# Blocks that depend on the context: kept as one float32 copy, split into two parts when they are loaded

## The reference, cut to what matters

```
# layer 0, for each batch
qh = (x @ wq + bq), kh = (ctx @ wk + bk), vh = (ctx @ wv + bv)     # 16 heads of 64
scores  = qh / 8 @ kh.T + 2 * bias
weights = softmax(scores)
out     = layernorm(weights @ vh (all heads side by side) @ wo + bo + x)
# layer 1: h = out + attn(ln(out)); h = h + attn(ln(h), context); h + geglu_ff(ln(h))
```

## Time and profile before

| | us |
|---|---|
| median of 3 runs (lowest, highest) | 3728.07 (3726.77, 3730.91) |
| the profiled execution | 3724.3 |
| span of its core | 3722.5 |
| busy PE / DVE / ACT / POOL | 2985.1 / 2187.8 / 1626.3 / 1329.6 |
| DMA moved in the span | 518.20 MB |

### The profile page before, as it was taken

The page is one execution under the profiler, slowest core; times in us unless marked ns, Lnnn a source line. Parts: engine busy times, 40 slices in busy tenths (PEclk is TensorE's granted clock), DMA queues, the critical chain, the costliest instruction groups (busy, mean ns, idle before and its releaser), DMA issues.

```text
span 3722.5 us, 50842 instructions
## 1 busy us (share of the span) xinstructions
PE 2985.1 (80%) x19712; PEld 2165.1 (58%) x19712; DVE 2187.8 (59%) x3575; ACT 1626.3 (44%) x2666; POOL 1329.6 (36%) x1025
## 2 busy tenths in 40 slices
PE   4447546769978988989968988889968888889999
PEld 3335433445656765655657755655757755665777
DVE  2335438768645558678446568578445568578431
ACT  3312117547522247457422247457322257367321
POOL 2142316544423225345332225345232334344221
PEclk8668765589989999989989989999989999999999
DMA  6883734322335431332344521322444421332334
GB/s 199 300 294 124 260 124 165 147 74 80 148 137 186 160 119 58 126 107 80 148 163 152 202 82 61 131 103 80 164 143 165 180 85 58 131 114 80 136 130 175
DMA packets 228974, 518.20 MB, mean 139 GB/s; under 512 B 96768, under 2 KB 113408, under 8 KB 206720
## 3 DMA queue, kind: packets, MB, share of 16 engines
q1 hardware_dynamic: 216320, 513.33, 38.0%
q10 hardware_dynamic: 12416, 1.62, 0.3%
HBM read 428.39 MB, written 82.31 MB: 137 GB/s over the span
## 4 chain that ended last, share of the span: by engine, by line
PE 58%; DVE 19%; ACT 6%; DMA 5%; issue 4%; POOL 4%; SPq 3%; ACTq 1%; POOLq 0%; DVEq 0%
PE psum L1581 17%; PE psum L1582 15%; PE psum L1583 15%; DVE mx L1461 6%; PE psum L1863 5%; DVE w1T L1480 3%; PE psum L1853 2%; PE psum L1877 2%; DVE den L1467 2%; DMA kept<-st_lo 1%; ACT e L1156 1%; ACT psum L1069 1%; DMA fw_lo<-pieces 1%; SPq L553 1%; POOL e L922 1%
## 5 line engine op out<-in xcount | busy, mean ns | idle before, releaser
L875 POOL TENSOR_SCALAR w1b<-e,rec 128x1024 f16<-128x1024 f32 x512 | 572.8, 1119 | 748.8 <-DVE rec L1469 657.3
L1461 DVE TENSOR_REDUCE mx<-psum 128x1 f32<-128x1024 f32 x512 | 624.6, 1221 | 183.2 <-PE psum L1854 179.2
L1156 ACT ACTIVATE e<-psum,nb,scale 128x1024 f32<-128x1024 f32 x512 | 617.1, 1205 | 16.8
L1863 PE MATMUL psum<-ident,w1b 128*128 128x128 f16 x4096 | 350.6, 235 | 149.5 <-DVE w1T L1480 136.0
L1581 PE MATMUL psum<-h_hi,fw_hi 128*128 128x512 f32 x1024 | 459.4, 449 | 8.1 <-DMA fw_lo<-pieces 5.7
L1863 PEld LDWEIGHTS psum<-ident,w1b 128*128 128x128 f16 x4096 | 262.8, 105 | 298.4 <-issue 254.2
L1582 PE MATMUL psum<-h_lo,fw_hi 128*128 128x512 f32 x1024 | 414.1, 404 | 0.0
L1583 PE MATMUL psum<-h_hi,fw_lo 128*128 128x512 f32 x1024 | 414.0, 404 | 0.0
L1480 DVE TENSOR_SCALAR w1T<-psum 128x1024 bf16<-128x1024 f16 x512 | 347.1, 678 | 38.7 <-PE psum L1863 36.6
L1581 PE MATMUL psum<-w_hi,ht_hi 128*128 128x512 f32 x640 | 264.0, 412 | 57.7 <-DVE e L1398 30.0
L1335 DVE TENSOR_TENSOR x<-psum,x 128x512 f32<-128x512 f32 x224 | 152.4, 685 | 266.2 <-PE psum L1583 266.2
(11 more groups left out here) (175 smaller groups left out, 5882.1 us busy)
## 6 DMA issues: line engine op xcount, KB each, us to landing
fw_hi<-pieces SPq DMA_DIRECT2D x192, 512.0 KB, 3.3
fw_lo<-pieces SPq DMA_DIRECT2D x192, 512.0 KB, 4.2
w_hi<-kept SPq DMA_DIRECT2D x80, 1024.0 KB, 5.0
w_lo<-kept SPq DMA_DIRECT2D x80, 1024.0 KB, 7.6
fbias<-in_fside_Bx16xSxS SPq DMA_DIRECT2D x64, 256.0 KB, 3.9
prep_raw<-in_L_xattn_ff_w SPq DMA_DIRECT2D x12, 1024.0 KB, 8.1
pieces<-prep_hi SPq DMA_DIRECT2D x24, 512.0 KB, 3.5
pieces<-prep_lo SPq DMA_DIRECT2D x24, 512.0 KB, 5.5
```

The source lines that it names most:

```text
L875: pool.tensor_scalar(w1b[u % NH][:], e1[u % NE][:], rec1[:, u % 8:u % 8 + 1], HALF, ALU.mult, ALU.add).then_inc(w1_ready.sem, 1)
L1156: act.activation(e1[s % NE][:], psum[:, i:i + 2, :].rearrange("p i n -> p (i n)"), ACT.Exp, bias=nb1[:, s % 4:s % 4 + 1], scale=scale[:, 0:1],
L1461: dve.tensor_reduce(mx1[:, s % 4:s % 4 + 1], psum[:, i:i + 2, :].rearrange("p i n -> p (i n)"), AX, ALU.max).then_inc(maxed1.sem, 1)
L1863: ins = pe.transpose(bank(bank_of(key)).bitcast(FP16)[:, k * P:k * P + P], w1b[u % NH][:, k * P:k * P + P], ident16[:])
```

## The change

The first stage stores M and N unsplit. For each group ACT copies two of the four banks and DVE the other two into one staging buffer (plain float32), and SP stores it once, 1 MB, into the DRAM tensor `mixed`. There are four staging buffers instead of two pairs, in the same space. The small weights stay split in `kept`.

When M or N is loaded in the main part, one DMA of 1 MB brings it to `w_mixed[s]`, which lies in the same memory as `w_lo[s]`. Then ACT copies it to `w_hi[s]` (one instruction of 128 x 2048, `block_high`) and POOL subtracts in place (four instructions of 128 x 512, `block_low`). PE waits for the last of these four. The order of loads and the slots are as before.

ACT does `block_high`: of M0 of chunk 0 and N0 of each even chunk after the split of x; of M1 after it in each cross; of N1 ahead of step 5; of M0 and N0 of an odd chunk at the very end of the cross of the even chunk, behind the last v1 bank; of M0 of the next batch ahead of the last norm of `middle`. POOL does `block_low`: of M0 of chunk 0 ahead of all else; of N0 of an even chunk behind fbias(0); of M1 behind fbias(1); of N1 half in step 5, half in step 6, each between fbias(i) and e(i-2); the others at the same ends as ACT.

```diff
+            def block_low(key, ks):
+                s = SLOT[key]
+                pool.wait_ge(block_hi_done.sem, block_hi_done.at(key))
+                for k in ks:
+                    pool.tensor_tensor(w_lo[s][:, k, :], w_mixed[s][:, k, :], w_hi[s][:, k, :].bitcast(F32), ALU.subtract
+                                       ).then_inc(block_lo_done.sem, 1)
...
                 host(0)
+                if n == 0:
+                    block_low((n, "M0"), range(4))
                 wait_filled(pool, ("xT", n, KT - 1))
                 add_bias(n, "L0_xattn_bo")
...
                         pool.tensor_tensor(f, f, crow[:, 512 * half:512 * half + 512], ALU.add).then_inc(fbias_ready.sem, 1)
+                        if i == 0 and n % NC == 0:
+                            block_low((n, "N0"), range(4))
+                        if i == 1:
+                            block_low((n, "M1"), range(4))
+                        if i in (5, 6):
+                            block_low((n, "N1"), range(2 * (i - 5), 2 * (i - 5) + 2))
...
+                if n % NC < NC - 1:
+                    block_low((n + 1, "M0"), range(4))
+                    block_low((n + 1, "N0"), range(4))
...
+                if n % NC == NC - 1 and n + 1 < CHUNKS:
+                    block_low((n + 1, "M0"), range(4))
                 pool.wait_ge(z_ready.sem, z_ready.at((3, n, NT - 1)))
...
+            def block_high(key):
+                s = SLOT[key]
+                wait_block(act, key)
+                act.activation(w_hi[s][:], w_mixed[s][:], ACT.Copy).then_inc(block_hi_done.sem, 1)
...
+                if n == 0:
+                    block_high((n, "M0"))
+                if n % NC == 0:
+                    block_high((n, "N0"))
+                block_high((n, "M1"))
                 for i in range(STEPS0 + 2):
+                    if i == 5:
+                        block_high((n, "N1"))
...
-                for part, st in enumerate((st_hi, st_lo)):
-                    sp.dma_start(kept[B * half:B * half + B, part, :, 512 * j:512 * j + 512].rearrange("b p n -> p b n"),
-                                 st[g % 2][:].bitcast(F32)).then_inc(group_stored[g % 2], 16)
+                sp.dma_start(mixed[B * half:B * half + B, :, 512 * j:512 * j + 512].rearrange("b p n -> p b n"), st[g][:]
+                             ).then_inc(group_stored[g], 16)
...
-                sp.dma_start(flat(w_hi[s]), kept[kept_row(key), 0]).then_inc(w_loaded[s], 16)
-                sp.dma_start(flat(w_lo[s]), kept[kept_row(key), 1]).then_inc(w_loaded[s], 16)
+                if name in MIXED:
+                    sp.dma_start(w_mixed[s][:].rearrange("p k n -> p (k n)"), mixed[mixed_row(key)]).then_inc(w_loaded[s], 16)
```

More of the change, by code:

```diff
@@ L261, in dram @@
             return nc.dram_tensor(name, shape, dt, kind="Internal").ap()
-        kept = dram("kept", (22, 2, P, 2048))
+        kept = dram("kept", (6, 2, P, 2048))
+        mixed = dram("mixed", (16, P, 2048))
         pieces = dram("pieces", (PIECES, 2, P, 1024))
@@ L311, in build @@
             + [(f"wq_{part}", [P, PAIRS, D], F32R) for part in ("hi", "lo")]
-            + [(f"st_hi{i}", [P, 4, 512], F32R) for i in range(2)] + [(f"st_lo{i}", [P, 4, 512], F32R) for i in range(2)]
+            + [(f"st{i}", [P, 4, 512], F32) for i in range(STAGED)]
             + [("crow_all", [P, B, H * SC], F32), ("k2q", [P, HG, B * SC], BF16), ("v2q", [P, 2, D], BF16)]
@@ L470, in wait_group_stored @@
         def wait_group_stored(eng, g):
-            dmas = sum(GROUP_DMAS[GROUPS[i][0]] for i in range(g % 2, g + 1, 2))
-            eng.wait_ge(group_stored[g % 2], 16 * dmas)
+            dmas = sum(GROUP_DMAS[GROUPS[i][0]] for i in range(g % STAGED, g + 1, STAGED))
+            eng.wait_ge(group_stored[g % STAGED], 16 * dmas)
         def wait_piece(eng, n, v):
@@ L536, in store_rows_M @@
             def store_rows_M(half, j):
-                g = GROUPS.index(("M", half, j))
+                g = GROUPS.index(("M", half, j)) % STAGED
+                wait_emptied(sp, ("M", half, j, 1, 0))
                 wait_emptied(sp, ("M", half, j, 1, 1))
-                for part, st in enumerate((st_hi, st_lo)):
-                    sp.dma_start(kept[B * half:B * half + B, part, :, 512 * j:512 * j + 512].rearrange("b p n -> p b n"),
-                                 st[g % 2][:].bitcast(F32)).then_inc(group_stored[g % 2], 16)
+                sp.dma_start(mixed[B * half:B * half + B, :, 512 * j:512 * j + 512].rearrange("b p n -> p b n"), st[g][:]
+                             ).then_inc(group_stored[g], 16)
             def store_rows_N(m):
-                g = GROUPS.index(("N", m))
+                g = GROUPS.index(("N", m)) % STAGED
+                wait_emptied(sp, ("N", m, 1, 0))
                 wait_emptied(sp, ("N", m, 1, 1))
                 r = 8 + B * (m // 4)
[L549 to L555, removed]
+                for h in range(2):
+                    for odd in range(2):
+                        dst = mixed[r:r + B, 64 * h:64 * h + 64, 512 * (m % 4):512 * (m % 4) + 512]
+                        sp.dma_start(dst.rearrange("(g o) p n -> o p g n", o=2)[odd],
+                                     st[g][64 * odd:64 * odd + 64, 2 * h:2 * h + 2, :]).then_inc(group_stored[g], 16)
             load_raw("k0a")
@@ L584, in _ @@
             keep_split("v1")
-            wait_group_stored(sp, len(GROUPS) - 2)
-            wait_group_stored(sp, len(GROUPS) - 1)
+            for i in range(STAGED):
+                wait_group_stored(sp, len(GROUPS) - STAGED + i)
             sp.wait_ge(small_stored.sem, small_stored.at("v2s"))
@@ L1143, in cross @@
                     prep_high(PREP[4 * n + 3])
+                if n % NC < NC - 1:
+                    block_high((n + 1, "M0"))
+                    block_high((n + 1, "N0"))
             def self_attention(n):
@@ L1296, in _ @@
             for j in range(KT):
-                low_rows_M(0, j)
+                copy_rows_M(0, j)
             for q in range(4):
```

114 lines of the change are left out of this document (60 added, 54 removed).

## The result

The changed kernel takes **3767.65 us** (median, 3761.3 to 3769.84), beside 3729.49 for the kernel before on the same chip: a ratio of 1.010, 95% interval 1.0083 to 1.0118. It is slower by about 38 us. The forecast was 3745, with 3712 to 3772 for 8 in 10. The direction and most of the chain of causes were right, the size was not: +17 was forecast, and the profiled executions differ by 42.7 (a span of 3765.2 against 3722.5).

The account below looks back on a forecast made before the run. The first stage was taken as bound by its stores, the main part as paced by PE with waits on others. Costs of +74.3 less 57 gave +17.3 us, forecast 3745 us, range 3712 to 3772 for 8 in 10.

Parts of the forecast that it names:

- Term 3: N1 in all eight chunks: its first half on POOL delays e(3), so PE waits; +3.3 us each.
- Term 2: Start of chunks 3, 5, 7: M0 and N0 on POOL delay fbias(0), then PE's clock is slow; +10.4 us each.
- Term 6: `middle`: DVE's z waits beside POOL's split of M0 for one piece, not four; +3 us for three batches.
- rival D: DVE locked out over all four POOL pieces, in z and the starts of seven crosses; +33, 3761 us; chance 0.08.
- Term 4: Start of chunks 2, 4, 6: N0 and M1 delay e(0) by 5.4 us, x comes 3.0 earlier; +2.4 each.
- Term 5: Starts of chunks 0 and 1: splits on POOL delay e(1) in chunk 0, +6.5 us; chunk 1 +0.
- Term 1: First stage: fewer bytes stored at 310 GB/s bring the last group's copy earlier; -57 us, bounds 36 to 67.
- A: Whole kernel: the forecast itself, 10 to 34 us longer, 3738 to 3762 us; chance 0.45.
- B: Odd chunks: POOL's backlog ahead of fbias(0) does not form or runs in idle time; -14, 3714 us; chance 0.17.
- C: First stage gains only 36 to 42 us, SP's issue and split waits replacing the stores; +35, 3763; chance 0.17.
- E: Whole kernel: costs of 55 to 65 us and the gain cancel within 7.5 us; 3728 us; chance 0.13.

Follow-up runs that it names:

- e3: Changed kernel with POOL's two halves of N1 put behind the scaling e(i-2) of steps 5 and 6 instead of ahead of it: 3729.69 us.
- e5: Changed kernel with POOL waiting for each 128x512 piece to finish before it issues the next: 3774.44 us.
- e1: Kernel before with only the new first stage; each block loaded by two DMAs as before, nothing split on load: 3659.56 us, ratio 0.9818 to the kernel before.
- e7: Changed kernel with ACT's rounding of M0 and N0 of chunks 3, 5 and 7 moved earlier among the last quantised banks: 3736.34 us.
- e8: Changed kernel with N1 behind e(i-2), even chunks' N0 and M1 ahead of x, odd chunks' M0 and N0 early, POOL waiting between pieces: 3682.07 us.
- e9: Changed kernel with N1 behind e(i-2), even chunks' N0 and M1 ahead of x, odd chunks' M0 and N0 early, no waits between pieces: 3675.44 us.
- e6: Changed kernel with each group of POOL pieces as one instruction (128x2048 for a block, 128x1024 for a half of N1): 3770.47 us.

## Why the prediction was wrong

The costs were forecast 31.7 us too low and the gain 7.2 us too low. The terms, by the shifts from step to step: N1 by the step from 5 to 6, the rest by what is left of each chunk.

```
term                              forecast   measured
1  first stage                      -57        -64.2
2  odd chunks 3, 5, 7               +31.2      +39.2
3  N1, eight chunks                 +26.4      +41.1
4, 6  even chunks, with middle      +10.2      +16.5
5  chunks 0 and 1                    +6.5       +9.1
sum                                 +17.3      +41.8
```

**Term 3 is the largest miss (14.7 us), mis-sized for the clock.** The wait was right to 0.1 us (3.3 forecast, 3.37 in the trace). Missing is what follows it: 1.8 us in each chunk of matmuls at 0.63 instead of 0.39 us, though the wait is only 3.4 us long. In Term 2 I charged for the slow clock and in Term 3 I did not, as if only waits of 10 us and more brought it. e3 settles it: without the wait 38.0 us come back (35.5 through the kernel before).

The row that Term 2 took the slow clock from was also read a little long: behind it the products stand 0.43 us apart from 407.25 to 410.83, which is 3.6 us and not 4.5.

**Term 2** (8.0 us): the late fbias was right (8.65 against 9.1). Missing is DVE held for 6.45 us over four pieces and the fbias. The sentence that failed is in Term 6: "it waits for one piece, not four", read from the single row of k2q; Term 2 charged nothing for DVE at all. It is true of `middle` (z 1.48 us, PE's wait 1.73, about +0.9 as forecast) and false at the start of an odd chunk, in two chunks of three. In chunk 7 the same two instructions of the same kernel stood like this:

```profile
2940.40 5.43 POOL L834 TENSOR_TENSOR w_lo<-mixed,w_hi 128x512 fp32r<-128x512 f32 x4
```

```profile
2940.68 1.53 DVE L1453 TENSOR_TENSOR e<-e,row_max 128x512 f32<-128x512 f32 x1
```

There step 0 to step 3 took 14.06 us, in chunks 3 and 5 17.11 and 17.18: being held costs 3.1 us a time, not 5.8, because the slow products hide the rest (e5). That is 6.2 of the 8.0 us. So rival D was a real mechanism, at another price: held over the whole run in two places, about 6 us in all. It explains a fifth of the miss in the costs, not most of it.

**Term 4** (6.3 us, with Term 6): from x to step 5 the three chunks are 5.7, 6.6 and 6.7 us late where 5.4 was forecast, 2.8 us in all. The stretch ahead of x, with z and the earlier x, was forecast at -2 each and shifted by +1.1, -0.2 and -3.4: 3.5 us. The credit for an earlier x was too large: PE's wait for x shrank by 1.7, 2.6 and 2.8 us and not by 3.0. The 2.9 us of chunk 6 that e1 shows too hide as much again, so that the even chunks really cost about 19 us.

**Term 5** (2.6 us): chunk 0's start cost 7.8 instead of 6.5, and what comes between it and N1 of chunk 1 1.3 instead of 0. Batch 0 was not tried by itself.

**Term 1** (7.2 us too small): the last copy came 62.0 us earlier and not 58, the 1 us taken off for SP's new block did not show, the tail behind the copy took 39.9 us instead of 41.5, and the last 0.5 come between the first load and x. The 310 GB/s were an average of the old stage, which left the queue idle between groups (23 GB/s from 100 to 110 us); the 17.8 MB of the prediction moved in 52.6 us (67.42 to 119.99), which is 339 GB/s. The 382 GB/s that it calls the best stretch was not: 120 to 130 and 170 to 180 us had 407 and 406. That its upper bound of 67 is near the -67.5 of e1 is luck, since in e1's trace the first stage ends 61.7 us earlier. The figure of the Trainium skill, page "DMA: Bandwidth & Descriptors", section "Anatomy of one DMA", 436 GB/s, is fitted there to DMAs that GpSimd issues, and these are issued by SP; no stretch of 10 us of these runs reached it, and 404 is the highest of the first stage after. Without this term's miss the direction would be the same.

**The rivals.** A, with the costs as forecast, reached from 3738 to 3762; the median lies 6 us outside it. B, faster, is false as to the changed kernel, but its condition (the backlog ahead of fbias(0) does not form) is what e7 makes true, for 31 us. C's total, 3763, lies near the median for another reason than its own: the first stage gained 64 us and not 36 to 42. E falls.

**What stays open.** Why DVE is held over a whole run of GpSimd instructions in some places and let in after one in others: in chunks 3 and 7 it arrived 0.30 and 0.28 us after the run began, and it was held in one and not in the other. In e3 it arrived in chunk 7 after the same 0.28 us and was held. With waits between the pieces it was never held (e5, e8), but I cannot say what decides it without them, nor why e7 and e9 have no such place in chunks 3, 5 and 7.

## What to carry to other kernels

Here work put on an idle engine cost by its place in that engine's order and not by its sum. The same 165 us on POOL made the kernel 1.0% slower in one order and 1.4% faster in another. Go through the engine's queue instruction by instruction, ask which one a faster engine waits for next, and put the new work right behind that one or into a wait for a DMA.

Ask of every new wait of the matmul engine whether slow matmuls follow it, and charge them: here a wait of 3.4 us cost 5.1. Shorter waits of the same kernel did not all bring them: behind this one the products stood 0.23 us apart.

```profile
1219.11 0.50 PE L1629 MATMUL psum<-w_hi,ht_hi 128*128 128x512 f32 x1 [2.29 <-POOL w_lo L834]
```

## What the runs showed of the hardware

- A VectorE instruction with two SBUF inputs, 0.69 us with GpSimd idle, took 6.45 to 6.47 us beside four GpSimd subtractions of 1.27 us and an addition that followed without a gap, in 9 of 16 like places of four traces; in the others it took 1.53. With a wait between the pieces it took at most 1.54 in all 8 (e5, e8), beside one GpSimd instruction of four times the length 4.81 (e6). z took 1.48 us beside four pieces and 4.71 beside the one. The Trainium skill, page "SBUF — State Buffer", section "SBUF: two separate sides", says that the port pair the two share is held exclusively for one whole instruction. e6 and z agree (4.81 and 4.71 us beside one of 4.5); the 6.45 us over five instructions do not.
- The clock fell for a short wait too: behind 3.37 us without matmuls the granted clock was 0.50, its lower level (1.2 of 2.4 GHz), and matmuls stood 0.43 us apart instead of 0.23, for 1.8 us of loss. Behind a wait of 2.29 us (1219.11) it was 1.00.
- The DMA queue moved 366 to 404 GB/s in the 10 us stretches from 100 to 150 us, at a share of 1.00 to 1.05, with stores and loads in turn.
- The first stage of one program differed by up to 3.4 us between profiled executions (the first transpose of x at 169.96 in the changed kernel, 170.86 in e5, 172.66 in e6 and 173.40 in e9, which have the same stage).
